# B's parts of a Mamba scan written to DRAM in 32-byte pieces instead of as masked tiles

## What is computed

```python
def _mamba(x, in_w, conv_w, conv_b, xproj_w, dt_w, dt_b, A_log, D_skip, out_w):
    ...
    dbl = xc @ xproj_w.T
    dt, Bm, Cm = (dbl[..., :r], dbl[..., r:r + n], dbl[..., r + n:])   # n = 16 states
    delta = jax.nn.softplus(dt @ dt_w.T + dt_b)
    dA = jnp.exp(delta[..., None] * A)
    dBu = delta[..., None] * Bm[:, :, None, :] * xc[..., None]

    def step(h, inp):
        da, dbu, c = inp
        h = da * h + dbu
        return (h, jnp.einsum('bdn,bn->bd', h, c))
    ...
```

## Time and profile before

| | us |
|---|---|
| median of three executions | 522.25 |
| lowest, highest | 522.17, 522.8 |
| the profiled execution | 521.73 |
| its span, first to last instruction | 519.9 |
| busy in the span: TensorE (PE) | 466.3 |
| VectorE (DVE) | 374.2 |
| ScalarE (ACT) | 233.6 |
| GpSimd (POOL) | 167.3 |

### The profile page before, as it was taken

One profiled execution on the slowest core, in us unless ns is written; L12 is line 12 of the kernel. 1 busy time (PEld: TensorE's weight loads), 2 busy tenths in 40 slices (PEclk: granted clock), 3 DMA queues, 4 the chain that ended last, 5 costly groups with the idle time before them and its releaser, 6 DMA issues.

```text
span 519.9 us, 6850 instructions
## 1 busy us (share of the span) xinstructions
PE 466.3 (90%) x1798; PEld 226.2 (44%) x1798; DVE 374.2 (72%) x711; ACT 233.6 (45%) x410; POOL 167.3 (32%) x163
## 2 busy tenths in 40 slices
PE   5989999999999989899697868988889888699997
PEld 2544555555565566444454421221222222285553
DVE  0056476665665669464799897999999999678655
ACT  1112212212312221376978856888888788211100
POOL 6000100100100021402442005888989898040000
PEclk9999999999999999999869976999999999999999
DMA  9992008600000000310217563556555664510000
GB/s 266 286 281 72 1 1 261 170 1 1 0 2 0 0 1 1 95 59 0 78 39 218 149 185 98 149 161 193 168 153 151 182 190 117 158 42 12 10 10 21
DMA packets 36072, 51.75 MB, mean 100 GB/s; under 512 B 5842, under 2 KB 26606, under 8 KB 36048
## 3 DMA queue, kind: packets, MB, share of 16 engines
q1 hardware_dynamic: 34896, 50.26, 33.1%
q10 hardware_dynamic: 1152, 1.19, 0.7%
HBM read 34.59 MB, written 16.52 MB: 98 GB/s over the span
## 4 chain that ended last, share of the span: by engine, by line
PE 31%; DVE 6%; SPq 6%; ACT 5%; DMA 5%; issue 4%; ACTq 0%; DVEq 0%; POOL 0%
PE ps L1964 6%; DMA brows<-bparts 4%; PE ps L1941 4%; PE ps L948 3%; PE ps L1627 3%; PE ps L955 3%; PE ps L1578 2%; PE ps L1600 2%; PE ps L1591 2%; SPq L1448 1%; PE ps L987 1%; SPq L1517 1%; PE ps L1609 1%; PE ps L994 1%; DVE da L1803 1%
## 5 line engine op out<-in xcount | busy, mean ns | idle before, releaser
L1771 POOL TENSOR_TENSOR gb<-da,hb 128x512 f32<-128x512 f32 x62 | 77.7, 1273 | 52.9 <-ACT da L1691 46.7
L1691 ACT ACTIVATE da<-da 128x512 f32<-128x512 f32 x128 | 79.3, 631 | 23.2 <-DVE da L1803 20.9
L1803 DVE TENSOR_TENSOR da<-ps,expA 128x512 f32<-128x512 f32 x128 | 84.4, 687 | 6.2 <-PE ps L1578 5.2
L305 PE MATMUL ps<-xbuf,convw 128*128 128x384 f32 (+1 forms) x240 | 82.9, 499 | 5.3 <-DMA convw<-in_conv_wT 5.3
L359 PE MATMUL ps<-wall,peT 128*128 128x512 f32 x144 | 67.8, 593 | 0.0
L305 PEld LDWEIGHTS ps<-xbuf,convw 128*128 128x128 f32 (+1 forms) x240 | 45.8, 194 | 37.4 <-ACTq L502 3.9
L1578 PE MATMUL ps<-drows,selb 96*128 96x512 bf16 x128 | 49.2, 406 | 9.2 <-DVE da L1803 5.3
L529 ACT ACTIVATE kvs<-ps 128x512 f32<-128x512 f32 x36 | 21.5, 598 | 57.3 <-PE ps L359 57.3
L1591 PE MATMUL ps<-urows,brows 96*128 96x512 bf16 x96 | 35.8, 400 | 11.5 <-DVE gb L1810 7.8
L521 ACT ACTIVATE peT<-ps 128x384 f32<-128x384 f32 x24 | 11.8, 492 | 75.9 <-PE ps L305 75.9
L1771 POOL TENSOR_TENSOR gb<-da,gb 128x512 f32<-128x512 f32 x30 | 37.8, 1278 | 0.0
(11 more groups left out here) (233 smaller groups left out, 783.6 us busy)
## 6 DMA issues: line engine op xcount, KB each, us to landing
xbuf<-in_xT SPq DMA_DIRECT2D x11, 768.0 KB
yscr<-yst SPq DMA_DIRECT2D x28, 208.0 KB
brows<-bparts SPq DMA_DIRECT2D x16, 240.0 KB, 3.1
drows<-dparts SPq DMA_DIRECT2D x15, 192.0 KB, 2.8
dparts<-pt SPq DMA_DIRECT2D x21, 128.0 KB, 2.4
uparts<-pt SPq DMA_DIRECT2D x18, 128.0 KB, 2.4
urows<-uparts SPq DMA_DIRECT2D x16, 144.0 KB, 2.8
inw<-in_in_wT SPq DMA_DIRECT2D x2, 1024.0 KB
```

The source lines that it names most:

```text
L305: mm = pe.matmul(bank(T_EMB + j % 2, 0, EN), convw[0:n, k, h * P:(h + 1) * P], xbuf[0:n, q, k, c * EN:(c + 1) * EN], start=(k == 0), stop= ...
L1691: act.activation(da_at(q, j), da_at(q, j), ACT.Exp, scale=-1.0).then_inc(da_ready, 1)
L1771: pool.tensor_tensor(gb_at(q, j), da_at(q, j), state, ALU.mult).then_inc({2: m2_done, 3: m3_done, 4: m4_done}[s_], 1)
L1803: dve.tensor_tensor(da_at(q, j), bank(j % 2), expA[:, j % 2, :], ALU.mult).then_inc(e_free, 1)
```

## The change

`bparts` gets another shape. It is now [kind][group][8 rows of 1280, and 16 x 8 elements more], so that the same memory can be read in two ways: as rows of 1280 (`brow_view`), and as rows of 1296 (`bdiag_view`), in which row i begins 16 elements further right than in the first. First all of it is filled with zeros, by 12 DMAs from `bz`, which is now as wide as a whole row. Once these have landed, `store_b` writes B's parts straight from the small tiles `bshi`, `bsmi` and `bslo` (128 x 5 x 16), down the diagonal: for each image and token 16 values, 32 bytes. The six masked products of GpSimd (three for each direction), their tiles and their semaphore are gone. `load_b` reads 12 blocks of 8 rows, which no longer lie one behind another. GpSimd waits for the zeros before it clears the unused half of `drows`, which now may lie where `bz` was.

```diff
@@ -111,7 +111,10 @@
-        bparts = nc.dram_tensor("bparts", (NG, 12, GB, 2 * L * P), BF16, kind="Internal").ap()
+        BW = 2 * L * P
+        bparts = nc.dram_tensor("bparts", (12, NG, GB * (BW + NS)), BF16, kind="Internal").ap()
+        brow_view = bparts[:, :, 0:GB * BW].rearrange("k g (i n) -> k g i n", n=BW)
+        bdiag_view = bparts.rearrange("k g (i n) -> k (g i) n", n=BW + NS)
@@ -844,7 +847,7 @@
-        bz = sb("bz", [P, L * P], BF16, ctx=pre)
+        bz = sb("bz", [P, BW], BF16, ctx=pre)
@@ -858,9 +861,6 @@
-        bhi = sb("bhi", [P, 2, L * P], BF16, ctx=pre)
-        bmi = sb("bmi", [P, 2, L * P], BF16, ctx=pre)
-        blo = sb("blo", [P, 2, L * P], BF16, ctx=pre)
@@ -1231,22 +1231,14 @@
             mask4 = maskb[:, :, :].unsqueeze(1).to_broadcast([P, L, GB, NS])
-            def spread(dst, src):
-                return pool.tensor_tensor(dst.rearrange("p (t g n) -> p t g n", t=L, g=GB),
-                                          src.unsqueeze(2).to_broadcast([P, L, GB, NS]), mask4, ALU.mult)
-
             def b_rest(d):
                 pool.wait_ge(bhi_ready, d + 1)
                 pool.tensor_tensor(brest[:, d, :, :], bct[:, d, :, R:R + NS], bshi[:, d, :, :], ALU.subtract).then_inc(bres_ready, 1)
-                spread(bhi[:, d, :], bshi[:, d, :, :]).then_inc(bd_ready, 1)
 
             def b_low(d):
                 pool.wait_ge(bmi_ready, d + 1)
                 pool.wait_ge(bres_ready, d + 1)
                 pool.tensor_tensor(bslo[:, d, :, :], brest[:, d, :, :], bsmi[:, d, :, :], ALU.subtract).then_inc(bslo_ready, 1)
-                spread(bmi[:, d, :], bsmi[:, d, :, :]).then_inc(bd_ready, 1)
-                pool.wait_ge(bslo_ready, d + 1)
-                spread(blo[:, d, :], bslo[:, d, :, :]).then_inc(bd_ready, 1)
@@ -1449,7 +1441,7 @@
         def load_b(sp, g, q):
-            sp.dma_start(brows[:, q], bparts[bass.ds(g, 1)].rearrange("g k i n -> (g k i) n")).then_inc(u_landed[q], 16)
+            sp.dma_start(brows[:, q], brow_view[:, bass.ds(g, 1)].rearrange("k g i n -> (k g) i n")).then_inc(u_landed[q], 16)
@@ -1459,14 +1451,16 @@
             def store_b(d):
-                sp.wait_ge(bd_ready, 3 * (d + 1))
-                for k, src in enumerate([bhi, bhi, bhi, bmi, bmi, blo]):
-                    sp.dma_start(bparts[:, 2 * k + d, :, d * L * P:(d + 1) * L * P], src[:, d, :]).then_inc(b_stored, 16)
+                sp.wait_ge(bslo_ready, d + 1)
+                for k, src in enumerate([bshi, bshi, bshi, bsmi, bsmi, bslo]):
+                    own = bdiag_view[2 * k + d, :, d * L * P:(d + 1) * L * P]
+                    sp.dma_start(own.rearrange("b (t p) -> b t p", p=P)[:, :, 0:NS],
+                                 src[:, d, :, :]).then_inc(b_stored, 16)
 
             sp.wait_ge(cleared, 1)
-            for d in range(2):
-                for k in range(6):
-                    sp.dma_start(bparts[:, 2 * k + d, :, (1 - d) * L * P:(2 - d) * L * P], bz[:, :]).then_inc(b_stored, 16)
+            for k in range(12):
+                sp.dma_start(brow_view[k], bz[:, :]).then_inc(b_stored, 16)
+            sp.wait_ge(b_stored, 16 * 12)
             store_b(0)
@@ -1475,7 +1469,7 @@
-            sp.wait_ge(bd_ready, 6)
+            sp.wait_ge(bslo_ready, 2)
             load_b(sp, 0, 0)
@@ -1749,6 +1743,7 @@
         def scan_gpsimd(pool):
             pool.wait_ge(xc_ready, 2 * DC)
             pool.wait_ge(bc_ready, 2)
+            pool.wait_ge(b_stored, 16 * 12)
             for q in range(2):
                 pool.memset(drows[0:KS // 2, q, :], 0.0).then_inc(cleared, 1)
```

More of the change, by code:

```diff
@@ L890, in tower @@
         cd_ready, cdT_ready, CT_ready = sem("cd_ready"), sem("cdT_ready"), sem("CT_ready")
-        bd_ready, bhi_ready, bres_ready, bmi_ready = sem("bd_ready"), sem("bhi_ready"), sem("bres_ready"), sem("bmi_ready")
+        bhi_ready, bres_ready, bmi_ready = sem("bhi_ready"), sem("bres_ready"), sem("bmi_ready")
         bslo_ready, b_stored = sem("bslo_ready"), sem("b_stored")
```

## The result

| | before | changed |
|---|---|---|
| median of 20 executions each, us | 521.91 | 522.79 |
| lowest, highest | 518.38, 523.72 | 520.73, 527.36 |
| the profiled execution | 521.73 | 524.13 |
| its span | 519.9 | 522.3 |

The ratio of the two is 1.004 with an interval of 1.0021 to 1.0059. On 521.91 us that is +2.1 us (1.1 to 3.1). The means, 521.49 and 523.49, say +2.0; the medians are only 0.9 apart, since single executions spread over 5 to 7 us. It is slower, by some 2 to 3.5 us.

A forecast was written before the change was run, and what follows sets the result against it. The bound was taken as a chain of waits over all engines, passing in the loop through SP and the brows load. Terms -1.3 + 3.8 = +2.5 us gave 524.2 profiled, 524.7 median; range 521.0 to 529.0.

The forecast's parts named there:

- The products and VectorE's stalls: Preparation: removing POOL's masked products frees VectorE of 1.64 us excess; -1.3 us, between 0 and -1.64.
- the cap of 1.3: Preparation: ScalarE can begin item 9 only 1.3 us earlier, after TensorE's dt_product(8) and its own work.
- the stall at 259.58: Preparation: delta_(1) held behind POOL's product; counted nothing, since VectorE then waits for ScalarE until 262.7.
- rival 4: Preparation: POOL's clearing of drows holds VectorE up as the products did; 526.0 us, counted within the forecast's 0.58.
- The zeros, at nothing: Twelve doubled DMAs at 214 us finish by 234, before anything needs them at 251; 0 us.
- `store_b`, at nothing: Preparation: six stores in 32-byte pieces, 6.2 or 14.7 us of data; taken as hidden, 0 us.
- Rival 3: Preparation: 32-byte writes jam the queue before store(2) to store(4), from 33 ns per piece; 529.7 us, chance 0.18.
- the doubling of the 26 ns: Preparation: read-modify-write doubles the small-packet price, six stores take 12 us, the sum grows some 3 us.
- +0.63 us per load: Scan loop: load_b costs +0.43 in SP's issue and +0.2 in transfer, on the chain six times; +3.8 us.
- The spread over 12 engines: Scan loop: 12 blocks use only 12 DMA engines, 8 rows each instead of 6; +0.2 us per load.
- Rivals 1: Scan loop: the load's form costs nothing, only VectorE's release remains; 520.9 us, chance 0.12.
- rival 2: Scan loop: the longer issue overlaps the transfer, leaving 0.2 us per load; -0.1 us, 522.2 us, chance 0.12.

The follow-up runs named there:

- six blocks: Kernel before, with only bparts rearranged so that load_b reads 6 outermost blocks of 16 rows; 543.25 us, ratio 1.043.
- The layout alone: Kernel before, with only the DRAM order of bparts changed so that load_b reads 12 blocks of 8 rows, masked products kept; 525.32 us, ratio 1.0048.
- the second timing: Changed kernel as it is, timed again against the kernel before; 524.33 us, ratio 1.0066.

## Why the prediction was right

**The products and VectorE's stalls: right in mechanism, too small in size.** "-1.3 us" was forecast, and from `absolute(5)` to `middle(4)` the traces have -1.6 (25.32 to 25.45 us in place of 26.98 to 27.11), the whole of the excess of 1.64 that was read from VectorE. The step that failed is the cap of 1.3, by 0.2 to 0.3. It stood on TensorE's `dt_product(8)` ending at 275.05 and on ScalarE's three us of work behind it. In the third trace of the changed kernel `dt_product(8)` ends 36.9 us after the first copy into `bct`, as before, and ScalarE begins item 9 1.5 us earlier all the same. In the first trace `dt_product(8)` itself ended earlier, at 274.16 (273.04 + 1.12), and item 9 began at 277.14. That part has nothing to do with the products: at `absolute(5)` the changed kernel was already 0.63 us ahead, through TensorE's clock. "Of the stall at 259.58 I count nothing" was right, and nothing is to be counted for the stall at `blo(0)` either. The -2.3 us at `middle(4)`, larger than any bound, is 1.7 of the products and 0.6 that the two executions differ by otherwise. The clearing of `drows` costs nothing where it is, as forecast, so rival 4 is out.

**The zeros, at nothing: right.** Twelve issues from 214 us on, longer than before (0.85 us each in place of 0.60, where the prediction took the same), landing in 4.3 us in the median, and `store_b(0)` came only at 251.4 (254.2 before, when it still waited for the products).

**`store_b`, at nothing: right, and further inside than the bounds.** Both prices for a small packet, 26 and 61 ns, were too high; it is 7.9 to 11.6 ns. `store(2)` went out at 277.89 in place of 278.98, and `high(5)` waited for nothing. Rival 3, the jam from 33 ns on, is out. So is the doubling of the 26 ns, which the prediction worked out as an estimate beside what the Trainium skill (DMA: Bandwidth & Descriptors, Specifications) says of transfers below 512 B, that they are a read-modify-write: no row here shows such a cost.

**`load_b`: the sum right, its two terms not.** +0.63 us per load was forecast, and a pair takes 17.09 us in place of 16.41, +0.68 (17.08 against 16.44, +0.64, in the second traces). The issue was taken at +0.43; it rose from 0.317 to 0.855, +0.54, over its bound of +0.48, which was the price of 14 blocks (L1509), and the first packet begins 0.66 us later. The spread over 12 engines was taken at +0.2; the packets take 2.2 to 2.3 us where they took 2.2, at most +0.1. One term was too small and the other too large by about the same. The spread is real where it is larger, with six blocks. The layout alone, which leaves all else but the issue of the zeros and of B's stores as it is, shows the whole price. Rivals 1 and 2 are out: the form isn't free, and the issue doesn't hide behind the transfer, since no packet begins before it is over.

**How often it is paid.** I counted six loads, those that stood in the chain. Two of three traces of the changed kernel have six as well and one has seven, but the gaps between them are what counts. Four pairs at the new length, +2.6 us, are shown, and +0.4 in the mean behind the last of them. In the pairs ahead of them the clock differs more than the form can. So the +3.8 was somewhat high: +3.1 shows over the whole loop.

**The sum.** -1.3 + 3.8 = +2.5 was forecast. The traces give -1.6 and about +3.1, and the timed runs +2.1 and +3.4. The sign and the places were right, and the size within the spread of the two measurements. Some of the agreement is luck. The two errors, 0.3 too little gained and up to 0.7 too much lost, would have put the forecast some 1 us too high. The agreement to 0.1 us with the profiled execution is not evidence: 1.1 us of its span's +2.4 lies behind the loop (81.72 against 80.63), at a granted clock of 0.74 against 0.87, where a second trace of the changed kernel has 1.00 and 79.30. And the median of 522.79 is 1.9 us below the 524.7 that was forecast for it, nearer to rival 2's 522.2. It is in the range only because that reached down to rival 1. What tells the forecast from rival 2 is the ratio, the second timing and the pairs of the loop, and not that median.

## What to carry to other kernels

A DRAM layout that is convenient for a few writes is paid for at every read: with an outermost count of 12 where there was 96, SP needed 0.5 us more to issue the load, its first packet began 0.66 us later, and the loop lost 0.64 to 0.68 us for each pair of groups. With a count of 6 the packets themselves took 1.3 us longer; with 16 they did not. Keep the pattern plain on the transfer that is issued often, and its outermost count from getting small, and put the odd form on the one that is issued rarely. And before shortening a DMA at the end of an engine's list, look for what stands ahead of it and isn't needed: moving the next weights' two loads behind the rows took the changed kernel from 0.4% slower to 0.7% faster than the kernel before. Last, before two single traces are subtracted, their granted clocks should be compared window by window: here up to 4 us of difference lay in stretches that the change does not touch.

## What the runs showed of the hardware that I had not expected

- Writes of 32 bytes to DRAM cost 7.9 to 11.6 ns per packet, less than half of what small reads cost at 95 us in this kernel (26 ns).
- SP's time to issue the same 240 KB rises with the form and not with the number of blocks: 0.317 us for 96 plain rows, 0.63 for 16 blocks of 6, 0.855 for 12 of 8, 0.81 for 6 of 16. The first packet follows 0.97, 1.42, 1.64 and 1.60 us after the issue begins.
- The dependence on the form has a good side: with the 12 kinds outermost (the layout alone), the stores of B's parts to `bparts` were issued in 0.45 us in place of 0.60 and landed in 2.1 in place of 2.5.
- A weight load of 96 x 128 with a step of ten 2-byte columns takes 138 ns in place of 98, and a ScalarE copy to such columns 0.56 us in place of 0.26.
